# Layer 2 of a four-layer network: TensorE convolves both channel halves, five of eight chunks of it inside the selective scan

## The reference

```
xin, z = split(einsum(x, in_proj_w))             # 256 channels each
xc = silu(depthwise_conv3x3(xin, conv_w) + conv_b)
xs = [xc by rows, xc by columns, and both reversed]      # 4 directions
dts_r, B, C = split(einsum(xs, x_proj_w))        # 8, 16 and 16 rows
dt = softplus(einsum(dts_r, dt_proj_w) + dt_proj_b)
for each position l:
    h = h * exp(dt[l] * A) + (dt[l] * xs[l]) * B[l]      # 256 x 16 states
    y[l] = sum over states(h * C[l])
y = sum of the four directions of (y + D * xs)
out = (layer_norm(y) * silu(z)) @ out_proj_w
```

## Time and profile before

| | |
|---|---|
| median of 3 runs | 40399.08 us (40380.85 to 40405.81) |
| the profiled execution | 40396.46 us, its span 40394.6 us |
| granted TensorE clock, mean | 0.875 |
| TensorE, VectorE, ScalarE, GpSimd busy in the span | 72%, 84%, 49%, 77% |
| one sample | some 2522 us, of it the scan of layer 2 some 1790 |

### The profile page before, as it was taken

The page is one execution under the profiler, slowest core; times in us unless marked ns, Lnnn a source line. Parts: engine busy times, 40 slices in busy tenths (PEclk is TensorE's granted clock), DMA queues, the critical chain, the costliest instruction groups (busy, mean ns, idle before and its releaser), DMA issues. The chain is left out here.

```text
span 40394.6 us, 270531 instructions
## 1 busy us (share of the span) xinstructions
PE 29251.1 (72%) x61476; PEld 11541.5 (29%) x61476; DVE 33936.9 (84%) x33869; ACT 19958.1 (49%) x37509; POOL 30996.0 (77%) x14776
## 2 busy tenths in 40 slices
PE   6777777777777777777777777777777777777777
PEld 3232232322323223232232322323223232232322
DVE  7969879698796987969879698796987969879698
ACT  4545545455454554545545455454554545545455
POOL 6949869498694986949869498694986949769497
PEclk8888888888888888888888888888888888888888
DMA  3424324243242432424324243242432424324243
GB/s 104 151 83 152 135 100 151 85 151 134 100 152 84 152 134 101 152 84 152 134 102 151 83 152 134 101 152 84 151 133 103 151 84 151 133 102 152 84 152 132
DMA packets 1387317, 5029.10 MB, mean 124 GB/s; under 512 B 164272, under 2 KB 165816, under 8 KB 1381440
## 3 DMA queue, kind: packets, MB, share of 16 engines
q1 hardware_dynamic: 1385536, 5010.20, 35.5%
HBM read 4938.25 MB, written 71.30 MB: 124 GB/s over the span
## 5 line engine op out<-in xcount | busy, mean ns | idle before, releaser
L662 PE MATMUL PS<-WORK,CST 128*128 128x512 f32 x36096 | 19792.8, 693 | 8395.9 <-POOL WORK L556 7606.2
L545 POOL TENSOR_TENSOR WORK<-WORK,XN 128x1024 f32<-128x1024 f32 x8192 | 19253.1, 2383 | 1.3
L662 PEld LDWEIGHTS PS<-WORK,CST 128*128 128x128 f32 x36096 | 7532.0, 220 | 20965.6 <-POOL WORK L556 10427.4
L1026 ACT ACTIVATE PS<-WORK,AN 128x512 f32<-128x512 f32 x17408 | 11307.0, 679 | 1984.9 <-DVE WORK L1576 1092.8
L1568 DVE TENSOR_TENSOR_SCAN PS<-PS,HST,WORK 128x512 f32<-128x512 f32 x8960 | 10975.2, 1272 | 45.4 <-ACT PS L1026 32.1
L1568 DVE TENSOR_TENSOR_SCAN WORK<-PS,HST,WORK 128x512 f32<-128x512 f32 x5376 | 6582.9, 1267 | 0.0
L556 POOL TENSOR_TENSOR WORK<-WORK,CWIDE 128x1024 f32<-128x1024 f32 x2048 | 4864.0, 2375 | 118.3 <-issue 65.2
L1026 ACT ACTIVATE HST<-PS 128x2 f32<-128x2 f32 x5152 | 858.6, 167 | 6586.2 <-DVE WORK L1576 6152.6
L632 POOL MEMSET XN<- 128x66 f32 x32 | 4.9, 154 | 5101.7 <-DVE SM L1414 5003.0
L1576 DVE TENSOR_TENSOR WORK<-PS,WORK 128x1024 f32<-128x1024 f32 x3072 | 3763.0, 1225 | 105.2
L1026 ACT ACTIVATE WORK<-PS 40x512 f32<-40x512 f32 (+2 forms) x1600 | 935.5, 598 | 3547.7 <-PE PS L662 2867.3
(11 more groups left out here) (158 smaller groups left out, 25260.5 us busy)
## 6 DMA issues: line engine op xcount, KB each, us to landing
XN<-xbc_rows SPq DMA_DIRECT2D x4096, 512.0 KB, 3.6
WORK<-xbc_rows SPq DMA_DIRECT2D x2816, 512.0 KB, 4.3
CWIDE<-xbc_rows SPq DMA_DIRECT2D x2304, 512.0 KB, 4.2
BIG<-in_spec_dram SPq DMA_DIRECT2D x32, 2048.0 KB, 12.3
X<-in_x_dram SPq DMA_DIRECT2D x68, 512.0 KB, 4.8
xbc_rows<-WORK SPq DMA_DIRECT2D x512, 64.0 KB, 3.1
out_dram<-X SPq DMA_DIRECT2D x64, 512.0 KB, 5.1
xbc_rows<-WORK SPq DMA_DIRECT2D x128, 32.0 KB, 1.6
```

The lines of the kernel that those rows point to most:

```text
L545: nc.gpsimd.tensor_tensor(S.both(S.Q[u % 6]), S.both(S.DU[u // SN % 2]), S.wide(S.BW, u).unsqueeze(1).to_broadcast([P, 2, NT]), MUL).then_ ...
L662: return nc.tensor.matmul(o, w, r, start=start, stop=stop)
L1026: return nc.scalar.activation(o, i, f, **k)
```

## The change

TensorE convolves both halves. `TAP2` gets nine more weights for the second half; they are made once in setup (diagonals by VectorE, spread over the partitions by nine matmuls with the `ones` matrix, then multiplied by the projection). VectorE's taps, the frame `PX3` and the projection `WX1` are gone.

Only chunk 0 is convolved before the first `rows`, chunk 1 before the first `steps`, chunk 2 after them. Chunks 3 to 7 are convolved inside the scan, in chunks `g` = 0 to 4 of direction 0 (`CONVOLVED` = 5): chunk `g + 3`, the first half at `n` = 9, 10, 11 into bank 7, three taps each, the second at `n` = 12 to 15 into bank 6 with 3, 2, 2 and 2 taps, each group ahead of the sum of that unit. ScalarE takes their silus at `n` = 0 of the next chunk, between two table loads. Since `XN` is needed for that, the B ring lies in the free part of `BIG2` during the first five chunks (`BW0`), and SP's first loads back into `XN` wait for the convolution. The side chain goes one unit later everywhere: `rows` at 1, 2, `split` at 3, `steps` at 4, 5, `softplus` at 5 to 10, `log_small` at 8 and 11, `sum_dt` at 9 and 12, `make_du` at 13.

```diff
+CONVOLVED = 5
...
+                s.BW0 = [BIG2[:, L // 2 + w * i + L // 2 * (i // 2):L // 2 + w * (i + 1) + L // 2 * (i // 2)] for i in range(4)]
...
+            def ring_b(s, g):
+
+                return s.BW0 if g < CONVOLVED else s.BW
...
@@ SyncE, spread_rows
+                        if i == 8 * CONVOLVED:
+                            e.wait_ge(conv_done, 2 * NCH - 2)
+                        if i == 8 * CONVOLVED + 3:
+                            e.wait_ge(conv_done, 2 * NCH)
-                        load(S.BW, S.b_loaded, i, 0)
+                        load(S.ring_b(i // 8), S.b_loaded, i, 0)
...
@@ GpSimd, scan2
-                                            S.wide(S.BW, u).unsqueeze(1).to_broadcast([P, 2, NT]),
+                                            S.wide(S.ring_b(u // SN), u).unsqueeze(1).to_broadcast([P, 2, NT]),
...
-                        if n == 8:
+                        if n == 9:
                             sum_dt(g + 1, 0)
-                        if n == 11:
+                        if n == 12:
                             sum_dt(g + 1, 1)
-                        if n == 12:
+                        if n == 13:
                             make_du(g + 1)
...
@@ TensorE, scan2
+                def taps(j, h, o, some):
+
+                    if j >= NCH // 2 - 1:
+                        e.wait_ge(xn_ready, 6)
+                    for t in some:
+                        r = mm(o, TAP2[:, ch(9 * h + t, P)], xn_tap(j, t), t == 0, t == 8)
+                    if some[-1] == 8:
+                        r.then_inc(conv_done, 1)
+
                 def rows(g, h):
 
+                    if h == 0 and g <= NCH:
+                        e.wait_ge(conv_act, 2 * min(g + 2, NCH) if g else 2)
...
                 for h in range(2):
+                    taps(0, h, bank(2 + h), range(9))
+                for h in range(2):
                     rows(0, h)
                 for h in range(2):
+                    taps(1, h, bank(h), range(9))
+                for h in range(2):
                     steps(0, h)
+                for h in range(2):
+                    taps(2, h, bank(4 + h), range(9))
                 for u in range(S.units):
                     g, n = u // SN, u % SN
                     if g + 1 < KDIR * NCH:
-                        if n < 2:
-                            rows(g + 1, n)
-                        if n in (3, 4):
-                            steps(g + 1, n - 3)
+                        if n in (1, 2):
+                            rows(g + 1, n - 1)
+                        if n in (4, 5):
+                            steps(g + 1, n - 4)
+                    if g < CONVOLVED:
+                        if n in (9, 10, 11):
+                            if n == 9:
+                                e.wait_ge(S.dt_steps, 4 * (g + 1) + 2)
+                            taps(g + 3, 0, bank(7), range(3 * (n - 9), 3 * (n - 8)))
+                        if n >= 12:
+                            if n == 12:
+                                e.wait_ge(S.dt_steps, 4 * (g + 1) + 4)
+                            taps(g + 3, 1, bank(6), (range(0, 3), range(3, 5), range(5, 7), range(7, 9))[n - 12])
+                    if u == 0:
+                        e.wait_ge(conv_act, 4)
...
@@ TensorE, block2
-                for j in range(NCH):
-                    if j >= 2:
-                        e.wait_ge(px_copied, j - 1)
-                    if j >= NCH // 2:
-                        e.wait_ge(xn_ready, 6)
-                    mm(bank(4 + j % 2), WX1[:, :], xn_mid(j)).then_inc(px_made, 1)
-                for j in range(NCH):
-                    if j >= 4:
-                        e.wait_ge(conv_act, j - 3)
-                    for t in range(9):
-                        r = mm(bank(j % 4), TAP2[:, ch(t, P)], xn_tap(j, t), t == 0, t == 8)
-                    r.then_inc(conv_done, 1)
-                e.wait_ge(conv_act, NCH)
-                e.wait_ge(dw_act, NCH)
...
@@ ScalarE, scan2
+                def silus(j, banks):
+
+                    for h in range(2):
+                        e.wait_ge(conv_done, 2 * j + h + 1)
+                        act(BIG1[:, h * L + j * NT:h * L + (j + 1) * NT], bank(banks[h]), ACT.Silu,
+                            bias=vec[f"cb{h}"]).then_inc(conv_act, 1)
...
+                    if u < 2:
+                        e.wait_ge(conv_act, 2 + 4 * u)
...
+                silus(0, (2, 3))
+                exp_and_log()
                 split(0)
                 for h in range(2):
                     for part in range(3):
                         softplus(0, h, part)
                 decays(0)
+                silus(1, (0, 1))
+                silus(2, (4, 5))
+                exp_and_log()
                 for u in range(S.units):
                     g, n = u // SN, u % SN
                     if u + 1 < S.units:
                         decays(u + 1)
+                    if n == 0 and 1 <= g <= CONVOLVED:
+                        silus(g + 2, (7, 6))
+                        exp_and_log()
                     if g + 1 < KDIR * NCH:
-                        if n == 2:
+                        if n == 3:
                             split(g + 1)
-                        if 4 <= n < 10:
-                            softplus(g + 1, (n - 4) // 3, (n - 4) % 3)
+                        if 5 <= n < 11:
+                            softplus(g + 1, (n - 5) // 3, (n - 5) % 3)
...
@@ VectorE, scan2 and setup
-                        if n == 7:
+                        if n == 8:
                             log_small(g + 1, 0)
-                        if n == 10:
+                        if n == 11:
                             log_small(g + 1, 1)
...
+            for t in range(9):
+                V.tensor_scalar(WORK[:, ch(t, P)], EYE, TC2[:, t:t + 1], float(P), MUL, MUL).then_inc(diag_made, 1)
```

More of the change, by code:

```diff
@@ L344, in program @@
         BD1, WU3 = BIG1[:, 2 * P:3 * P], BIG1[:, 3 * P:4 * P]
-        PX3 = WORK[:, 0:PW * PW].rearrange("p (h w) -> p h w", w=PW)
-        DW = [WORK[:, PW * PW + NT * i:PW * PW + NT * (i + 1)] for i in range(2)]
         Z2 = BIG1[:, :2 * L].rearrange("p (d l) -> p d l", l=L)
@@ L404, in program @@
                  (WO0[:, :], d["wo0"]), (FW0[:, :], d["ffw0"]), (w3(FW1[:, :], a=4), d["ffw1"]),
[L405 to L406 removed]
+                 (BIG1[:, 0:P], d["inpx"]), (BIG1[:, P:2 * P], d["inpx1"]), (TC2[:, :], d["tc2"]), (WZ2[:, :], d["inpz"]),
+                 (TAP2[:, 0:9 * P], d["cw2"].partition_broadcast(P)), (WO2[:, :], d["wo2"]),
                  (DTW2[32:32 + RANK, :], d["dtw2"]), (DTB2[:, :], d["dtb2"]), (AN2[:, :], d["al2"]),
@@ L641, in _ @@
                     frame(0)
-                    for edge in (PX3[:, 0, :], PX3[:, PW - 1, :], PX3[:, 1:PW - 1, 0:1], PX3[:, 1:PW - 1, PW - 1:PW]):
-                        nc.gpsimd.memset(edge, 0.0).then_inc(px_frame, 1)
                     scan2()
@@ L1012, in _ @@
             mm(bank(7)[:, 1:2], cst["cen"], vec["ffb1"]).then_inc(pe_setup, 1)
+            e.wait_ge(diag_made, 9)
+            for t in range(9):
+                r = mm(bank(t // 4)[:, ch(t % 4, P)], cst["ones"], WORK[:, ch(t, P)])
+            r.then_inc(taps_spread, 1)
             e.wait_ge(vec_ready, 1)
@@ L1132, in block1, with exp_and_log @@
                 rstd(NCH - 1)
+            def exp_and_log():
+                e.preload_act_table_set("natural_log_exp_and_others")
             def scan2():
                 S = S2
+                def silus(j, banks):
[3 more added lines that the diff above has]
+                            bias=vec[f"cb{h}"]).then_inc(conv_act, 1)
                 def split(g):
@@ L1209, in scan2 @@
                         decays(u + 1)
+                    if n == 0 and 1 <= g <= CONVOLVED:
+                        silus(g + 2, (7, 6))
+                        exp_and_log()
                     if g + 1 < KDIR * NCH:
-                        if n == 2:
+                        if n == 3:
                             split(g + 1)
-                        if 4 <= n < 10:
-                            softplus(g + 1, (n - 4) // 3, (n - 4) % 3)
+                        if 5 <= n < 11:
+                            softplus(g + 1, (n - 5) // 3, (n - 5) % 3)
                     if S.of(u)[1] < NCH - 1:
                         carry(u)
-            def exp_and_log():
-                e.preload_act_table_set("natural_log_exp_and_others")
             def block2():
-                for j in range(NCH):
-                    e.wait_ge(px_made, j + 1)
-                    act(PX3[:, 1 + ROWS * j:1 + ROWS * (j + 1), 1:1 + HW], w3(bank(4 + j % 2), a=ROWS),
-                        ACT.Copy).then_inc(px_copied, 1)
-                for j in range(NCH):
-                    e.wait_ge(dw_done, j + 1)
-                    act(BIG1[:, L + j * NT:L + (j + 1) * NT], DW[j % 2], ACT.Silu, bias=vec["cb1"]).then_inc(dw_act, 1)
-                    e.wait_ge(conv_done, j + 1)
```

(29 more changed lines are left out.)

7 lines of the change are left out of this document (2 added, 5 removed).

## The result

The changed kernel takes **41,590.87 us** (median of four runs) against 40,402.26 us for the kernel before on the same chip. One of its runs (45,196.81) shows a granted clock of 0.663 where the others have 0.87; it counts in the median and is left out of the ratio, which is **1.0293** with a 95% interval of 1.0273 to 1.0313. The kernel is 2.9% slower. I had forecast 0.8% faster.

The account below looks back on a forecast made before the run. GpSimd was taken to bound the scan and TensorE layer 2's convolution. Per sample -38.7 + 8.4 + 0.5 + 8.4 = -21.4, x 16 = -342, with setup -339: 40,060 us, range 39,860 to 40,270.

Parts of the forecast that it names:

- The start of layer 2: Before the scan: fewer taps ahead of the first scan bring it 38.7 us earlier per sample.
- Setup: Once, in setup: nine small VectorE operations and one more product over 1152 columns cost 3.7 us.
- What the taps inside the scan cost: Chunks 0 to 4: 18 more taps each on TensorE make `take_y` late, costing 8.4 us per sample.
- the signs that I had named for being wrong: VectorE waiting for ScalarE at unit 2 or state 10; in chunks 0-4, clock under 0.9 or periods of 60 and more.
- The 3 taps ahead of state 9 fit in: Chunks 0 to 4: three TensorE taps finish before GpSimd has weighed state 9, at 613.9.
- the taps fill just the gaps of 3 to 6 us before states 9, 12 and 14: Chunks 0 to 4: taps occupy TensorE's gaps, an argument against its clock falling.
- What the shift by one unit costs: Side chain, scan chunks: GpSimd waits 0.6 us in 14 column chunks, 8.4 us per sample, plus 0.5 for 17 others.
- The rival of the clock: Chunks 0 to 4: TensorE's clock falls to its lower level under the taps: 42,150 us; chance 0.07.
- The silus reach VectorE: Five chunks' starts: a ScalarE table load behind its wait delays VectorE, +86 us: 40,146 us; chance 0.12.
- The shift costs in all chunks: State 10's `decays` is ready just when VectorE wants it, 0.5 us in 17 more chunks: 40,196 us; chance 0.11.
- Nothing is given back: Scan: it stays at GpSimd's pace, so the whole gain at the start remains: 39,784 us; chance 0.10.

## Why the prediction was wrong

- **The start of layer 2**: forecast 38.7 us a sample, measured 38.9. Setup: 3.7 and 4.4. Right.
- **What the taps inside the scan cost**: forecast 8.4 us a sample. Measured as the changed kernel's first six periods against those of the shift alone, (53.7 + 297.0) - (53.3 + 286.3) = 11.1 in sample 1, and 9.4 in the mean of the 16 samples. The size is nearly right, in part by luck, with two misses inside. The periods were to be 57.5, with about 3 us of VectorE's wait before `take_y`; they are 57.8 to 60.4, with 4.4 to 5.6 of wait in chunks 1 to 4, and the two over 60 are among the signs that I had named for being wrong. "The 3 taps ahead of state 9 fit in" is true, but they do not fill the wait, and the sum behind it ran slow. And "the taps fill just the gaps of 3 to 6 us before states 9, 12 and 14" was wrong for state 9, where 2.61 stay.
- **What the shift by one unit costs**: the step that failed. Forecast 8.4 + 0.5 us a sample, with some 17 as the bound; measured 1,689 / 16 = 106. I computed the room at one place, `sum_dt`, and took the rest of the shift to be free. The part that I had looked at cost 20 (1.0 and not 0.6 in a column chunk, 0.4 and not none in the others), a size missed by a factor of two, and the wait was at the first `sum_dt` and not at the second. What was not looked at at all are two moves: `make_du` behind state 12's weighing (55 us a sample when alone, 50 to 67 of the 90 in the chunks without taps), and the row products out of `take_y`'s slot (7 to 24 of the 90). The first puts the longest wait of TensorE, 6.16 us, ahead of the last two sums, which then take 6.35 us and not 3.70. I had noted how the clock stands behind gaps (12 records in 7.11 after one), and that VectorE's whole reserve is 0.9 us ahead of `take_y`. I did not ask which sums would be behind the longest gap after the move.
- **The rival of the clock** had the right cause in the wrong place. I put it under the taps, beside which the mean clock is 0.92 and not 0.88, and gave it 0.07. It decided in the chunks without taps. The periods that it gave, 83 us, were seen nowhere.
- **The silus reach VectorE**: not in the changed kernel. Behind the load of 555.21 + 1.28 the next operation started at 556.50. So the drain of some 1380 ns, which the Trainium skill (ScalarE: Activation LUTs, What ACT_TABLE_LOAD costs) puts on top of a load, does not show here. With the taps behind the sums the rival happened. **The shift costs in all chunks**: the sign was right, through other waits.
- **Nothing is given back**: no.

The measured parts add up nearly to the time of the changed kernel: -622 (start) + 1,689 (shift) + some 178 (taps) + 4 (setup) = +1,249, against 1,189 measured. With the taps at their mean over the samples, 9.4 and not 11.1, it is 28 less. Where the other 32 us lie stays open.

## What to carry to other kernels

Where an engine's clock falls in its long waits, a move that keeps all work and all ends the same can still cost: ask which of its instructions stands behind the longest wait after the move, and who waits for that one. A mean clock or a busy share doesn't show it; the durations of one shape, by place in the loop, do. When a side chain is shifted, price every one of its instructions on every queue: what cover it leaves (here TensorE's wait for `take_y`) and what it now stands in front of. And a gap ahead of a critical matmul is the place for work that must be done anyway.

## What the runs showed of the hardware

- Four matmuls of no use ahead of the last sums took some 1,090 us off a kernel of 41,591 us, by keeping the granted clock up: eight records took 3.70 us behind them at a granted clock of 1.00, and 6.35 at 0.58 without.
- One GpSimd instruction of 2.3 to 2.9 us, moved behind a drive and a weighing, cost 886 us in 40,391, with no engine given more to do.
- Two row products moved one unit on held ScalarE for 10.68 us in its queue (5.79 before), and cost 934 us.
